# Two pairs of steps change places in the preparation, the step-size products read all 128 rows, and TensorE starts on a tile of ones

## What is computed

```python
xn = layernorm(x)                                   # (8, 512, 128)
xz = einsum('ed,bld->bel', in_proj_w, xn)           # 256 channels of x, 256 of z
for way in (forward, backward):                     # the same on xz reversed in time
    u = silu(causal_conv4(x) + bias)
    x_dbl = x_proj_w @ u                            # 8 step-size rows, 16 rows of B, 16 of C
    delta = softplus(dt_proj_w @ x_dbl[:8] + dt_bias)   # the step size
    dA = exp(delta * A); dBx = delta * B * u        # 16 states a channel
    h = scan(dA, dBx); y = sum_n(h * C) + D * u
    out += y * silu(z)
y1 = out_proj_w @ out
logits = -|xn - keys|^2 + rw @ xn + rb              # 16 experts, the best 4 of each token
y2 = sum_k softmax(top4)_k * (w2 @ gelu(w1 @ xn + b1) + b2)
return x + y1 + y2
```

## Time and profile before

| | |
|---|---|
| median of 3 runs | 1203.09 us |
| the three runs | 1200.37, 1203.09, 1204.73 us |
| the profiled execution: time | 1202.14 us |
| the profiled execution: span, first to last instruction | 1200.2 us |
| mean granted TensorE clock, 1.0 being 2.4 GHz | 0.925 |
| busy, share of the span | PE 79%, PEld 63%, DVE 90%, ACT 76%, POOL 73% |

### The profile page before, as it was taken

The page is one execution under the profiler, slowest core; times in us unless marked ns, Lnnn a source line. Parts: engine busy times, 40 slices in busy tenths (PEclk is TensorE's granted clock), DMA queues, the critical chain, the costliest instruction groups (busy, mean ns, idle before and its releaser), DMA issues. The chain is left out here.

```text
span 1200.2 us, 21505 instructions
## 1 busy us (share of the span) xinstructions
PE 948.7 (79%) x5691; PEld 752.3 (63%) x5764; DVE 1083.1 (90%) x1402; ACT 910.8 (76%) x1647; POOL 874.9 (73%) x530
## 2 busy tenths in 40 slices
PE   5267788854789888988898888889888888897872
PEld 5133243323678767877777677777777767776762
DVE  7886788849999999999999989999999999698952
ACT  2037887777799987989898888889898987878720
POOL 1077868773579878987897788789878878785562
PEclk9987877776899999999999999999999998899985
DMA  9924445568556866776676668667766766554455
GB/s 314 325 82 156 176 154 218 186 250 294 178 168 170 228 184 168 199 198 178 162 218 185 190 151 228 166 170 201 203 171 165 230 177 170 141 146 144 118 108 152
DMA packets 151298, 222.64 MB, mean 185 GB/s; under 512 B 36028, under 2 KB 97756, under 8 KB 146276
## 3 DMA queue, kind: packets, MB, share of 16 engines
q1 hardware_dynamic: 124036, 202.16, 52.6%
q0 software_dynamic: 27136, 19.02, 11.1%
HBM read 159.74 MB, written 65.52 MB: 188 GB/s over the span
## 5 line engine op out<-in xcount | busy, mean ns | idle before, releaser
L748 POOL TENSOR_TENSOR arena<-arena 128x1024 f32<-128x1024 f32 x227 | 494.2, 2332 | 147.3 <-DVE arena L1390 131.7
L1390 DVE TENSOR_TENSOR_SCAN arena<-arena,ps 128x512 f32<-128x512 f32 x512 | 601.0, 1205 | 0.1
L934 ACT ACTIVATE arena<-delta,a_neg 128x511 f32<-128x511 f32 x512 | 338.2, 723 | 4.2 <-issue 2.2
L733 POOL DMA_INDIRECT acc_d<-yrows,tags x160 | 255.2, 1595 | 54.3 <-issue 36.1
L1083 PE MATMUL ps<-ident,arena 128*128 128x128 f32 x2048 | 275.8, 279 | 7.0 <-POOL arena L748 4.7
L1378 DVE TENSOR_TENSOR ps<-du,ps 128x512 f32<-128x512 f32 x384 | 253.8, 676 | 10.1 <-issue 5.8
L1083 PEld LDWEIGHTS ps<-ident,arena 128*128 128x128 f32 x2048 | 238.1, 144 | 17.6 <-POOL arena L748 4.7
L1112 PE MATMUL ps<-w,arena 128*128 128x128 f32 x1248 | 177.6, 286 | 10.5 <-DVE arena L1390 5.4
L715 POOL DMA_INDIRECT slots_d<-arena,pos x128 | 154.2, 1205 | 42.1 <-issue 40.6
L1104 PE MATMUL ps<-rowsT,w 128*128 128x256 f32 x640 | 159.1, 393 | 8.9 <-ACT arena L885 7.1
L1112 PEld LDWEIGHTS ps<-w,arena 128*128 128x128 f32 x1248 | 155.2, 194 | 15.1 <-ACT yrows L880 5.3
(11 more groups left out here) (141 smaller groups left out, 944.5 us busy)
## 6 DMA issues: line engine op xcount, KB each, us to landing
arena<-c_d SPq DMA_DIRECT2D x128, 512.0 KB
w<-w_dram SPq DMA_DIRECT2D x80, 258.0 KB
w<-w_dram SPq DMA_DIRECT2D x80, 256.0 KB
rows<-slots_d SPq DMA_DIRECT2D x80, 130.0 KB
slots_d<-delta SPq DMA_DIRECT2D x5, 2015.0 KB, 20.2
delta_d<-arena SPq DMA_DIRECT2D x8, 1024.0 KB
du_d<-delta SPq DMA_DIRECT2D x8, 1024.0 KB
delta<-delta_d SPq DMA_DIRECT2D x8, 1024.0 KB, 7.3
```

Of the source, the lines that this page charges most:

```text
L733: pool.indirect_dma_start(acc_d, bass.IndirectOffsetOnAxis(ap=tags[:, j, a, 0:1].bitcast(I32), axis=0), yrows[:, j % W_RING, a, :], None, ...
L748: nc.gpsimd.tensor_tensor(state[:, q % H_RING], state[:, q % H_RING], c_rows[:, r % C_RING], ALU.mult).then_inc(s["prod_done"], 1)
L934: nc.scalar.activation(decay[:, q % DA_RING, j, lo:lo + L - 1], delta[:, par, dh, lo:lo + L - 1], ACT.Exp, scale=a_neg[:, dh, 2 * g + j:2 ...
L1390: nc.vector.tensor_tensor_scan(state[:, q % H_RING, j, way], decay[:, q % DA_RING, j, way], b_ps[:, ROW[q, j], j, way], 0.0, ALU.mult, ALU ...
```

## The change

- ACT: the square comes before the logarithm, in every round.
- DVE: in rounds 1 to 6 the last of the four taps of the next convolution comes after `small`, the first three stay ahead of it. In round 0 the whole convolution stays ahead; round 7 has none.
- PE: the step-size products take all 128 rows of `dtw` and `xdbl` in place of 9. POOL zeroes `dtw` at the start, and SP waits for that ahead of the weights' loads. ACT's first `prepare` waits for DVE's fill of `xdbl`.
- PE: 80 bf16 matmuls of 128x128 ones by 128 columns of ones stand at its very start, into PSUM bank 0, whose first use comes later. They wait for the tile of ones, which POOL now fills as its first instruction, in place of DVE.
- DVE: the two small `drop` products move from after the first convolution to the routing part of the head.

```diff
+WARM = 80
@@ SP
+            sp.wait_ge(s["dtw_zeroed"], 1)
             for dst, src in ((chan[:, :, :], chan_in), (inw, inw_in), (xproj, xproj_in), (dtw[BR:BR + NR], dtw_in),
@@ POOL
+            nc.gpsimd.memset(ones[:, :], 1.0).then_inc(s["ones_set"], 1)
+            nc.gpsimd.memset(dtw, 0.0).then_inc(s["dtw_zeroed"], 1)
             nc.gpsimd.memset(delta[:, :, :, :], 0.0).then_inc(s["zero_v"], 1)
@@ ACT prepare(b)
                 wait(act, s["c_out"], 16 * b)
+                if b == 0:
+                    act.wait_ge(s["ones_ready"], 1)
...
-                act.wait_ge(s["exp_ready"], b + 1)
                 wait(act, s["sum_ready"], ND * b)
-                nc.scalar.activation(ln1p, mag, ACT.Ln, scale=LN_SCALE, bias=ln_bias[:, 0:1]).then_inc(s["ln_ready"], 1)
                 act.wait_ge(s["small_ready"], b + 1)
                 nc.scalar.activation(fit, small, ACT.Square, scale=SQ_SCALE, bias=fit_bias[:, 0:1]).then_inc(s["square_ready"], 1)
+                act.wait_ge(s["exp_ready"], b + 1)
+                nc.scalar.activation(ln1p, mag, ACT.Ln, scale=LN_SCALE, bias=ln_bias[:, 0:1]).then_inc(s["ln_ready"], 1)
@@ PE
+            pe.wait_ge(s["ones_set"], 1)
+            for k in range(WARM):
+                nc.tensor.matmul(ps[:, 0, 0:P], ones[:, :], ones[:, :], start=True, stop=True)
@@ PE prepare(b)
-                        last = nc.tensor.matmul(ps[:, DT_BANK + d * NH + h, :], dtw[BR:BR + NR + 1, d, h * P:(h + 1) * P],
-                                                xdbl[BR:BR + NR + 1, d, :], start=True, stop=True)
+                        last = nc.tensor.matmul(ps[:, DT_BANK + d * NH + h, :], dtw[:, d, h * P:(h + 1) * P], xdbl[:, d, :],
+                                                start=True, stop=True)
@@ DVE
-            nc.vector.memset(ones[:, :], 1.0)
...
+            for k in range(2):
+                last = nc.vector.tensor_scalar(drop[0:BR, k, :], consts[0:BR, C_ID:C_ID + BR], consts[0:BR, C_PART + k:C_PART + k + 1],
+                                               None, ALU.mult)
+            last.then_inc(s["drop_ready"], 1)
             dve.wait_ge(s["logit_ps"], 1)
...
-            def convolve(b):
+            def convolve(b, taps):
...
-                for k in range(KC):
+                for k in taps:
...
-                    convolve(b + 1)
+                    convolve(b + 1, range(KC) if b == 0 else range(KC - 1))
...
                 nc.vector.tensor_scalar(small, mag, SMALL, None, ALU.min).then_inc(s["small_ready"], 1)
+                if 0 < b < BATCH - 1:
+                    convolve(b + 1, range(KC - 1, KC))
...
-            nc.vector.memset(xdbl[BR:P], 1.0)
-            for k in range(2):
-                last = nc.vector.tensor_scalar(drop[0:BR, k, :], ...)
-            last.then_inc(s["drop_ready"], 1)
+            nc.vector.memset(xdbl[BR:P], 1.0).then_inc(s["ones_ready"], 1)
```

More of the change, by code:

```diff
@@ L434, in build_kernel @@
             late_in1 skip_in0 skip_in1 decay_ready b_ready dbx_done scan_done prod_done v_prod_done summed y_free m0_ready m0_free m1_ready m1_free gelu_done
-            b2_in b2_split b2_out turn_ps turned scaled
+            ones_set dtw_zeroed ones_ready b2_in b2_split b2_out turn_ps turned scaled
             mixed_out mixed_in sp_step pool_step acc_ready out_done"""
@@ L1274, in _ @@
             nc.vector.tensor_scalar(a_neg[:, :, :], a_neg[:, :, :], -1.0, None, ALU.mult)
-            def convolve(b):
-                dve.wait_ge(s["xpad_ready"], b + 1)
-                wait(dve, s["u_ready"], ND * b)
-                for k in range(KC):
+            def convolve(b, taps):
+                if taps[0] == 0:
+                    dve.wait_ge(s["xpad_ready"], b + 1)
+                    wait(dve, s["u_ready"], ND * b)
+                for k in taps:
                     for q in range(DH):
@@ L1343, in _ @@
             start = done[0]
-            convolve(0)
+            convolve(0, range(KC))
             nc.vector.memset(parts_p[BR:P], 0.0)
-            nc.vector.memset(xdbl[BR:P], 1.0)
-            for k in range(2):
-                last = nc.vector.tensor_scalar(drop[0:BR, k, :], consts[0:BR, C_ID:C_ID + BR], consts[0:BR, C_PART + k:C_PART + k + 1],
-                                               None, ALU.mult)
-            last.then_inc(s["drop_ready"], 1)
+            nc.vector.memset(xdbl[BR:P], 1.0).then_inc(s["ones_ready"], 1)
             for b in range(BATCH):
```

## The result

The change makes the kernel slower: 1212.13 us (median of 11 runs, 1207.98 to 1217.58) against 1200.89 for the kernel before in the same session (11 runs). The ratio is 1.0095, 95% interval 1.007 to 1.012. I had forecast 1190.5 and a range of 1184 to 1200. The profiled execution of after took 1209.07 us, its span is 1207.2.

What follows compares the result with a forecast made beforehand. The preparation's rounds were taken as bound by a chain of ACT and PE in turn, set by PE's clock. 10.5 + 1.9 = 12.4 us off 1202.14 gave 1189.7, written 1190.5 for the median; range 1184 to 1200.

Steps and rivals of the forecast that it cites:

- 128 rows: Step-size products on PE: full height keeps the clock and removes ACT's excess idle, 12.06 less 1.5, so 10.5 us.
- Rival 1: Step-size products: height doesn't matter to the clock, only 1.9 us are left, 1201.2, the same; 14%.
- Square first: ACT: nothing by itself in rounds 0 to 6, but a condition of the 128-row gain; 1.9 us in round 7.
- the loop of 22.3 us: Preparation rounds: DVE's chain L1311 to L1330, convolution, bound and ACT's square, the next bound under the old order.
- The bound ahead of the last tap: DVE, preparation rounds: 2.7 us of taps move behind the bound, no work added, neither DVE nor ACT waits long.
- Rival 5: End of preparation: the scatter becomes the limit, SP waits for experts' weights, at most 3 us charged, 1193.5; no separate chance.
- The head: Kernel start: fills, moved products and 80 matmuls cost zero; PE done by 10 us, ahead of its first tile at 12.5.
- rivals 3 and 4: Head: ones' full clock carries over, 1185.5, 5%; or ones run late, 1212.7, 4%, another 4% for 1194 to 1200.

Runs made afterwards that it cites:

- the kernel before with fewer DMAs: The kernel before with 35 of the 128 scatter DMAs, the first round whole and one DMA of each other round: 1201.93 us, ratio 0.9978.
- the kernel with the logarithm first and the short reads: The kernel after with ACT's logarithm ahead of the square and one-column PSUM reads ahead of the first fit and first sum: 1192.7 us, 0.9933.
- the kernel with inputs from PSUM: The kernel after with DVE's fit and sum taking their first input from PSUM, giving wrong step sizes: 1191.4 us, ratio 0.9892.
- direction by direction: The kernel after with DVE's fit, sum and positive part of one direction ahead of the other's: median 1208.19 us, no ratio.
- after with fewer DMAs: The kernel after with 35 of the 128 scatter DMAs, the first round whole and one DMA of each other round: 1188.98 us, ratio 0.9868.

## Why the prediction was wrong, step by step

**128 rows.** Right in kind; the size is not settled. Forecast 10.5 us; measured alone, 13.2 in seven rounds against before, and 6.9 against the kernel before with fewer DMAs, whose 9 rows kept the clock in more rounds. In after ACT's idle time ahead of L810 and L819 went from 15.0 + 9.3 to 10.7 + 0.0: 13.6 us where I had counted 12.06. I had put all of the 9.3 down to PE, where the earlier trace rows gives it 4.4; all of it went. The 1.5 us that I took off for a clock lost more often did not appear: the wait before the copies of x_dbl went from 13.4 to 12.5. Rival 1 is out, as far as 9 and 128 rows go: with the height alone changed, the skip products took 3.60 us in every round and the skip copy waited for nothing, where it had waited 9.3 us.

**Square first.** Right in round 7. From the last exponential to the last store it is 16.79 us in before (259.98 to 276.77) and 14.95 in after (243.06 to 258.01), 1.84 for the 1.9 forecast. With the logarithm first it is 16.80 again. In the earlier rounds it was to give nothing by itself, and with the logarithm first rounds 2 to 6 are indeed as short, 21.27 to 21.69 us from the last store of one to that of the next. I had made it a condition of rounds shorter than the loop of 22.3 us as well. That was the tap's move instead: with the square first and the convolution whole the rounds take 22.2.

**The bound ahead of the last tap.** Here the prediction failed. I costed the edit at nothing, "no work is added", "neither waits long". The seven rounds take 151.42 us in after (91.64 to 243.06), 17.0 less than in before; height alone gave 13.2, so 3.8 are left for the order. Most rounds of after take 21.30 us, those with the convolution whole 22.2. So of the 18.8 us the height gave 13.2, the order in the rounds 3.8, and the square in the last round 1.8. The first two come from single traces and are no firmer than that: the kernel without the ones, with the same height and order as after, took 155.20 us for the seven rounds. But with the square first the edit also closes the pause of 3.52 us ahead of L1311. I had called that pause DVE's slack and asked only whose work it would delay on DVE and ACT. Nobody waited for DVE then, but POOL's scatter lived on it.

**Rival 5, the scatter becomes the limit.** The right place, with a wrong price. I took the scatter's last DMA at 271.84 as fixed and charged at most 3 us (for a wait of SP of up to 5.3, which I wrote as 5.4) for a preparation that catches up with it. The scatter moved 24.6 us the other way, and the first step that pays isn't the experts' weights but POOL's first product, which stands behind the scatter in POOL's own queue. That product had 13.50 us of room in before, so even a fixed end would have kept back some 5 of the 18.8 us. The sign of it that I had named, POOL's first product no earlier, is what came.

A trace of it was in the earlier trace rows: the DMA of 1.96 us at 269.88 lies under the two instructions that follow DVE's fits. Plainer still is POOL's copy at 165.72, 4.26 us where the shortest takes 0.24: it ended at 169.98, 0.10 us after DVE's run of taps and small values had ended. I read neither as a hold.

The Trainium skill ("SBUF — State Buffer", "SBUF: two separate sides") has VectorE and GpSimd share a pair of SBUF ports under an exclusive lock, held for the whole instruction, and keeps GpSimd from writing the descriptors of its DMAs while VectorE runs in a two-port mode. The same page of the Trainium skill ("Who interferes with whom") has an instruction with two SBUF inputs contend with a GpSimd instruction that reads SBUF, and reports that `tensor_tensor` did not stall a DMA. POOL's copy, which reads SBUF, agrees. The DMAs do not: the fit and the sum, with two SBUF inputs, held one for 4.90 to 5.57 us (it took 0.96 once both read PSUM), and the product with u, a `tensor_tensor`, held one for 2.96. They differ in the length too: a DMA lay under four instructions of 1.2 us each.

**The head.** Right. The 80 pairs end at 7.2 us, 78 ns a pair, and the routing loads stay at 333 ns; rivals 3 and 4 fall. Lines L973 and L989 of after, min/median/max:

```profile
L973 PE MATMUL ps<-ones x80: 219/219/314, 1.0 to 7.0; 128*128 128x128 bf16 x80
...
L989 PEld LDWEIGHTS ps<-arena x64: 333/333/338, 14.7 to 33.6; 128*128 128x128 f32 x64
```

So in the profiled pair the terms of the sum came out at 18.8 us for 12.4, and the kernels in which the scatter is let through or cut short stand at 1191.4, 1192.7 and 1188.98, near where I had put this one. That nearness is in part luck, as the terms were 18.8 us in one pair of traces and 9.5 in the other. What failed is the step that left the scatter's end fixed and gave the lost pause of DVE no price.

## What to carry to other kernels

Before you call an engine's idle time slack, look at what other engines do in it: here a pause of DVE was the time in which POOL's DMAs got through. When two chains meet, as the preparation and the scatter do, a gain in one is worth only the room that the other leaves, so work out the other's end again under the new schedule, DMA by DMA, instead of taking it from the old trace. A pause of a quarter of a microsecond, or a short read of PSUM, between instructions with two SBUF inputs can be worth more than the time it takes.

## What the runs showed that I had not expected

- A DMA on POOL's queue is held by DVE's 128x1024 f32 instructions with two SBUF inputs for as long as they follow each other without a pause ahead of them: 4.90 to 5.57 us for a DMA of 0.96. It ends 0.91 us after the first one that reads PSUM begins. Under the 128x512 taps of the convolution (L1305), which also have two inputs from SBUF, most DMAs take 1.02 us. Yet one that began 0.05 us after the taps had begun took 7.30 us in the kernel with the logarithm first and the short reads, and one that began 0.06 after 6.16 in the kernel with inputs from PSUM. Like those under fit and sum, they ended 0.83 us after DVE's run had ended. Why a few of these are held and most are not is open.
- POOL's own small copies are held as well: in the kernel with 128 rows alone one took 7.38 us at 111.03. It ended at 118.41, 0.10 us after DVE's taps and small values.
- A pause of DVE ahead of the run changes the whole run: after 0.25 us or more, each held DMA gets through by the next pair of instructions, and the DMA under the product with u, some 7 us later, takes at most 1.84 us in place of 2.96. The runs don't show why a pause has an effect that late.
- Products over 9 rows cost the clock in some rounds, products over 128 rows in none, at the same number of instructions and columns: the skip products behind them take 3.60 us in all 80 rounds of the ten traces with 128 rows, and in one round of eight of before.
- The step from round 0 to round 1 is 21.30 us in after, 26.22 in before, 27.80 with the logarithm first, 30.19 direction by direction, counted at ACT's exponential. The order alone doesn't set it: it is 24.54 in after with fewer DMAs, and 21.30 with the logarithm first and the short reads. What sets it I did not try.
